# The convolution of the next chunk moved between the two scans, the second C spread early in every turn, the first stretch reordered

## The reference, cut to what matters

```
proj = xn @ W_in + b_in;  x_ssm, x_gate = split(proj)
x_conv = silu(causal depthwise conv of x_ssm, 4 taps, + conv_b)
B, C = split(x_conv @ W_bc + b_bc);  dt = softplus(x_conv @ W_dt + b_dt)
h[t] = h[t-1] * exp(dt[t] * A) + dt[t] * x_conv[t] * B[t]      (16 states per feature)
y[t] = sum over the states of h[t] * C[t] + x_conv[t] * D
mamba = LN((y * silu(x_gate)) @ W_out + b_out + xn)

gates = softmax(xn @ gate_w); the best two of 8 experts, weights normalised
h_e = gelu(LN(xn @ w1_e + b1_e));  y_e = h_e @ w2_e + b2_e
moe = LN(sum of the two weighted y_e + xn)
```

## Time and profile before

| what | value |
|---|---|
| median of 3 runs | 1748.9 us (1748.78 to 1751.86) |
| the profiled execution, its own time | 1749.06 us |
| its span, first to last instruction | 1747.1 us |
| granted TensorE clock, mean | 0.951 of full |
| busy: PE, DVE, ACT, POOL | 1517.9, 1511.7, 1293.8, 1002.6 us |

### The profile page before, as it was taken

The page is one execution under the profiler, slowest core; times in us unless marked ns, Lnnn a source line. Parts: engine busy times, 40 slices in busy tenths (PEclk is TensorE's granted clock), DMA queues, the critical chain, the costliest instruction groups (busy, mean ns, idle before and its releaser), DMA issues.

```text
span 1747.1 us, 27926 instructions
## 1 busy us (share of the span) xinstructions
PE 1517.9 (87%) x6796; PEld 936.7 (54%) x6796; DVE 1511.7 (87%) x2454; ACT 1293.8 (74%) x2431; POOL 1002.6 (57%) x586
## 2 busy tenths in 40 slices
PE   5898549898989999999989898989999999995688
PEld 3665125565555655655556565655566565653233
DVE  5677569999999999999999999999999998941897
ACT  3545358788878787887878787888787878756687
POOL 2677736556656665565656565666665655732233
PEclk9777769999999999999999999999999999999799
DMA  7999643343334333333333433433443433325695
GB/s 227 329 292 347 238 161 83 85 103 98 88 98 107 95 109 90 102 87 98 101 98 90 110 90 100 100 98 87 102 112 87 108 78 91 79 45 140 214 289 172
DMA packets 178468, 228.34 MB, mean 131 GB/s; under 512 B 45967, under 2 KB 145048, under 8 KB 178331
## 3 DMA queue, kind: packets, MB, share of 16 engines
q1 hardware_dynamic: 137422, 166.02, 31.4%
q0 software_dynamic: 25584, 35.54, 10.9%
q10 hardware_dynamic: 15328, 25.20, 4.2%
HBM read 146.17 MB, written 80.53 MB: 130 GB/s over the span
## 4 chain that ended last, share of the span: by engine, by line
DVE 30%; PE 29%; ACT 16%; issue 15%; DMA 5%; ACTq 3%; SPq 1%; DVEq 0%; POOLq 0%
PE psX L1032 6%; DVE area L1358 6%; PE psY L1053 5%; DVE area L1371 4%; DVE area L1367 4%; PE psH L1020 3%; PE psT L1080 3%; ACT area L673 3%; ACT h_T L710 3%; DMA area<-L_attn_x 3%; DVE area L1388 2%; DVE more L1423 2%; PE psT L1008 2%; ACTq L694 2%; PE psT L1110 2%
## 5 line engine op out<-in xcount | busy, mean ns | idle before, releaser
L553 POOL TENSOR_TENSOR area<-area,more 128x1024 f32<-128x1024 f32 x256 | 599.8, 2361 | 490.6 <-DVE area L1367 246.0
L1388 DVE TENSOR_TENSOR area<-area,psD 128x1024 f32<-128x1024 f32 x256 | 310.2, 1212 | 0.5 <-issue 0.2
L1020 PE MATMUL psH<-w_sb,ffn_xT 128*128 x540 | 266.4, 617 | 45.3 <-DVE area L1402 38.0
L537 POOL DMA_INDIRECT expert_d<-y_out,meta x135 | 220.6, 1634 | 80.1 <-ACT y_out L689 33.5
L1053 PE MATMUL psY<-ident,area 128*128 128x128 f32 x2048 | 251.1, 276 | 0.0
L673 ACT ACTIVATE area<-area,A_sb 128x512 f32<-128x512 f32 x256 | 170.0, 712 | 81.8 <-DVE area L1371 43.5
L1053 PEld LDWEIGHTS psY<-ident,area 128*128 128x128 f32 x2048 | 222.7, 141 | 13.6 <-DVE area L1388 0.4
L1032 PE MATMUL psX<-w_sb,h_T 128*128 x720 | 182.8, 399 | 7.5 <-issue 6.5
L667 ACT ACTIVATE psD<-area,A_sb 128x512 f32<-128x512 f32 x256 | 174.8, 683 | 16.5 <-POOL area L544 9.5
L1020 PEld LDWEIGHTS psH<-w_sb,ffn_xT 128*128 128x128 f32 x540 | 96.2, 194 | 149.3 <-issue 149.1
L524 POOL DMA_INDIRECT sorted_x<-area,place x128 | 127.8, 998 | 77.3 <-DVE place L1336 39.8
(11 more groups left out here) (190 smaller groups left out, 2700.1 us busy)
## 6 DMA issues: line engine op xcount, KB each, us to landing
more<-B_rows_d SPq DMA_DIRECT2D x128, 512.0 KB, 4.0
xin<-sorted_x SPq DMA_DIRECT2D x135, 128.0 KB, 2.0
area<-L_attn_x SPq DMA_DIRECT2D x8, 1024.0 KB, 6.8
xnT_d<-w_sb ACTq DMA_DIRECT2D x16, 512.0 KB, 6.5
expert_d<-area ACTq DMA_DIRECT2D x8, 1024.0 KB
ssm_d<-w_sb ACTq DMA_DIRECT2D x16, 512.0 KB
w_sb<-L_ffn_w SPq DMA_DIRECT2D x16, 512.0 KB
more<-ssm_d SPq DMA_DIRECT2D x16, 512.0 KB, 3.9
```

The lines of the kernel that those rows point to most:

```text
L537: pool.indirect_dma_start(out=expert_d, out_offset=bass.IndirectOffsetOnAxis(ap=meta_tok[:, t % RING, :], axis=0), in_=y_out[:, t % 2, :], ...
L553: pool.tensor_tensor(inflow[:, k], dtx, B_rep[par][:, k].rearrange("p (a t) -> p a t", a=1).to_broadcast([P, KD, CHUNK]), ALU.mult).then_i ...
L1020: nc.tensor.matmul(psH[:, :], ffn_xT[:, k, :], w1_sb[:, bass.ds(e, 1), k, :].rearrange("p o h -> p (o h)"), start=(k == 0), stop=False)
L1388: V.tensor_tensor(h, h, C_rep[k].rearrange("p (a t) -> p a t", a=1) .to_broadcast([P, KD, CHUNK]), ALU.mult).then_inc(S[f"hC{k}_done"], 1)
```

## The change

On VectorE `convolve(g, 0)` moves from the end of turn 0 to between `scan0_of` and `scan1_of` of turn 0, and `convolve(g, 1)` with `pad_left` from the end of turn 1 to between `gate` and `scan1_of` of turn 1. On TensorE `spread_C1` (and `transpose_x` in turn 1) take in turns 0 and 1 the place that they have in all others. In the first stretch the ranks come after tile 1 instead of tile 5; `pick` is written behind the other constants and has a semaphore of its own; the memset of `h_T` goes. The scatters are counted in three groups: GpSimd's and VectorE's first scan now wait for tiles below LAST (61 of 64), and only the loads of sorted tokens wait for the rest. SP issues four loads of w2, `store_B(0)`, the padding rows, both `load_B`, and then five loads of w1.

```diff
...
 END_RING = 8
-CONSTS = 22 + 5
+CONSTS = 17 + 5
 
...
         h_norm2 = scan_area.take(HIDDEN)
+        LAST = -(-scan_area.at // ROW)
         scan_more = Carve(sb("more", [P, 7300]), 7300)
...
             xin_loaded xin_T xT_copied h_ready bn_done var_ready hln_ready rstd_ready norm_done hT_done gelu_done
-            y_ready y_copied y_stored pool_consts
+            y_ready y_copied y_stored pool_consts pick_ready scattered_last
             e_bias e_chain e_var e_ln e_root e_scale e_norm e_gain e_gain1 e_sum""".split()
...
             sp.dma_start(xT_in, xnT_d[0].rearrange("p (k t) -> p k t", k=KD)).then_inc(S["xT_loaded"], 16)
+            def store_B(g):
+                sp.wait_ge(S["bc_taken"], g + 1)
+                sp.dma_start(B_rows_d[bass.ds(g, 1)].rearrange("o n t -> (o n) t"), bc_f[0:STATE, :]).then_inc(S["B_stored"], 16)
+
+            def load_B(p, g, pr):
+
+                if pr == 0:
+                    sp.wait_ge(S["B_stored"], 16 * (g + 1))
+                if p >= 2:
+                    sp.wait_ge(S["dbx_done"], 2 * p)
+                sp.dma_start(B_rep[pr % 2], B_rows_d[bass.ds(g, 1), 2 * pr:2 * pr + 2, :].to_broadcast([P, 2, CHUNK])
+                             ).then_inc(S[f"B_loaded{pr % 2}"], 16)
+
+            sp.wait_ge(S["xT_store0"], 16 * TURNS + 16)
+            sp.wait_ge(S["xT_store1"], 16 * TURNS + 16)
+            sp.wait_ge(S["ssm_store0"], 16 * TURNS + 16)
+            sp.wait_ge(S["ssm_store1"], 16 * TURNS + 16)
+            for dst, src in w2_loads[:w2_after]:
+                sp.dma_start(dst, src).then_inc(S["w_ffn"], 16)
+            store_B(0)
             sp.wait_ge(S["pads_found"], 1)
...
                 sp.dma_start(sorted_x[bass.ds(row, P), :], xin[:, :]).then_inc(S["pad_fill"], 16)
+            load_B(0, 0, 0)
+            load_B(1, 0, 1)
             sp.wait_ge(S["tables_ready"], 1)
-            sp.wait_ge(S["xT_store0"], 16 * TURNS + 16)
-            sp.wait_ge(S["xT_store1"], 16 * TURNS + 16)
-            sp.wait_ge(S["ssm_store0"], 16 * TURNS + 16)
-            sp.wait_ge(S["ssm_store1"], 16 * TURNS + 16)
-            for dst, src in w1_loads[:w1_after] + w2_loads[:w2_after]:
+            for dst, src in w1_loads[:w1_after]:
                 sp.dma_start(dst, src).then_inc(S["w_ffn"], 16)
...
 
-            def store_B(g):
-                sp.wait_ge(S["bc_taken"], g + 1)
-                sp.dma_start(B_rows_d[bass.ds(g, 1)].rearrange("o n t -> (o n) t"), bc_f[0:STATE, :]).then_inc(S["B_stored"], 16)
-
-            def load_B(p, g, pr):
-
-                if pr == 0:
-                    sp.wait_ge(S["B_stored"], 16 * (g + 1))
-                if p >= 2:
-                    sp.wait_ge(S["dbx_done"], 2 * p)
-                sp.dma_start(B_rep[pr % 2], B_rows_d[bass.ds(g, 1), 2 * pr:2 * pr + 2, :].to_broadcast([P, 2, CHUNK])
-                             ).then_inc(S[f"B_loaded{pr % 2}"], 16)
-
             def store_mamba(c):
...
             load_ssm(1)
-            store_B(0)
-            load_B(0, 0, 0)
-            load_B(1, 0, 1)
-            sp.wait_ge(S["scattered"], 16 * 2 * (TILES - FIRST))
+            sp.wait_ge(S["scattered"], 16 * 2 * (LAST - FIRST))
+            sp.wait_ge(S["scattered_last"], 16 * 2 * (TILES - LAST))
             sp.wait_ge(S["pad_fill"], 16 * EXPERTS)
...
                 pool.memset([ident, before][k][:, :], 0.0 if k == 0 else 1.0).then_inc(S["pool_consts"], 1)
-            pool.memset(pick[:, :, :], 0.0).then_inc(S["pool_consts"], 1)
-            pool.wait_ge(S["pool_consts"], 5 + 3)
+            pool.wait_ge(S["pool_consts"], 5 + 2)
             pool.affine_select(out=ident[:, :], in_=ident[:, :], compare_op=ALU.not_equal, fill=1.0, base=0,
...
 
-            for r in range(PARTS):
-                pool.wait_ge(S["pool_consts"], 5 + 5 + r)
-                pool.affine_select(out=pick[:, :, :], in_=pick[:, :, :], compare_op=ALU.not_equal, fill=1.0,
-                                   base=-(BC * r + STATE), pattern=[[-1, STATE], [0, P]], channel_multiplier=1
-                                   ).then_inc(S["pool_consts"], 1)
             pool.memset(ones[:, :], 1.0).then_inc(S["pool_consts"], 1)
...
             pool.memset(half_neg[:, :], -0.5).then_inc(S["pool_consts"], 1)
-            pool.memset(h_T[:, :, :, :], 0.0).then_inc(S["pool_consts"], 1)
             pool.memset(ones_e, 1.0).then_inc(S["pool_consts"], 1)
...
             pool.memset(not_first[:, :, 0:1], 0.0).then_inc(S["pool_consts"], 1)
+            pool.memset(pick[:, :, :], 0.0).then_inc(S["pick_ready"], 1)
+            for r in range(PARTS):
+                pool.wait_ge(S["pick_ready"], 1 + r)
+                pool.affine_select(out=pick[:, :, :], in_=pick[:, :, :], compare_op=ALU.not_equal, fill=1.0,
+                                   base=-(BC * r + STATE), pattern=[[-1, STATE], [0, P]], channel_multiplier=1
+                                   ).then_inc(S["pick_ready"], 1)
 
...
                         out=sorted_x, out_offset=bass.IndirectOffsetOnAxis(ap=place[:, i, k:k + 1], axis=0),
-                        in_=row_all[:, i, :], in_offset=None).then_inc(S["scattered_first" if i < FIRST else "scattered"], 16)
+                        in_=row_all[:, i, :], in_offset=None).then_inc(S["scattered_first" if i < FIRST else "scattered" if i < LAST else "scattered_last"], 16)
 
...
             pool.wait_ge(S["zero_fill"], 16 * 2)
-            pool.wait_ge(S["scattered"], 16 * 2 * (TILES - FIRST))
+            pool.wait_ge(S["scattered"], 16 * 2 * (LAST - FIRST))
             pool.wait_ge(S["xn_stored"], 16 * TURNS)
...
 
-            RANKS_AFTER = GROUP - 3
+            RANKS_AFTER = 1
 
...
             pe.wait_ge(S["tables_ready"], 1)
+            pe.wait_ge(S["pick_ready"], 1 + PARTS)
             spread_C0(0, 0, 0, 0)
...
                                 transpose_sum(c)
-                            early_C = pr != CONV_TURN - 1
-                            if early_C:
-                                spread_C1(u + 1, state[1], par)
+                            spread_C1(u + 1, state[1], par)
                             if u >= 2:
                                 down(u - 2)
-                            if not early_C:
-                                spread_C1(u + 1, state[1], par)
                             if pr == 0:
...
                         else:
-                            early_C = pr != CONV_TURN
-                            if early_C:
-                                transpose_x(u + 2)
-                                if go_on:
-                                    spread_C1(u + 1, state[1], par)
+                            transpose_x(u + 2)
+                            if go_on:
+                                spread_C1(u + 1, state[1], par)
                             pe.wait_ge(S["gelu_done"], u)
...
                                 task(TASKS[pr], g)
-                            if not early_C:
-                                transpose_x(u + 2)
-                                spread_C1(u + 1, state[1], par)
                             if u >= 2:
...
             finish_dt(0, 0)
-            dve.wait_ge(S["scattered"], 16 * 2 * (TILES - FIRST))
+            dve.wait_ge(S["scattered"], 16 * 2 * (LAST - FIRST))
             dve.wait_ge(S["xn_stored"], 16 * TURNS)
...
                             gate(c, ahead)
+                        if pr == CONV_TURN - 1 and more:
+                            convolve(g, 0)
+                        if pr == CONV_TURN and more:
+                            convolve(g, 1)
+                            pad_left(half == 0)
                         if pr == BC_TAKEN + 1 and more:
...
                         times_C(u, pr * 2, 0, half)
-                        if pr == CONV_TURN - 1 and more:
-                            convolve(g, 0)
-                        if pr == CONV_TURN and more:
-                            convolve(g, 1)
-                            pad_left(half == 0)
             for u in range(MAMBA_TURNS, FFN_TURNS):
...
```

More of the change, by code:

```diff
@@ L390, in load_B, with load_tile, load_chunk @@
                              ).then_inc(S[f"B_loaded{pr % 2}"], 16)
+            sp.wait_ge(S["xT_store0"], 16 * TURNS + 16)
[5 more added lines that the diff above has]
+            store_B(0)
+            sp.wait_ge(S["pads_found"], 1)
+            for e in range(EXPERTS):
+                row = sp.value_load(pad_row[0:1, e:e + 1], min_val=0, max_val=EXPERTS * REGION * P - P)
+                sp.dma_start(sorted_x[bass.ds(row, P), :], xin[:, :]).then_inc(S["pad_fill"], 16)
+            load_B(0, 0, 0)
+            load_B(1, 0, 1)
+            sp.wait_ge(S["tables_ready"], 1)
+            for dst, src in w1_loads[:w1_after]:
+                sp.dma_start(dst, src).then_inc(S["w_ffn"], 16)
+            def load_tile(t, slot):
+                row = sp.value_load(row_of[0:1, bass.ds(t, 1)], min_val=0, max_val=BLOCKS * P - P)
+                if not (isinstance(t, int) and t == 0):
```

(5 more changed lines are left out.)

14 lines of the change are left out of this document (removed).

## The result

The changed kernel takes 1783.37 us (median of 4 runs, 1777.85 to 1786.75), the kernel before 1749.31 us beside it (4 runs, 1748.78 to 1751.86): a ratio of 1.0189, 95% interval 1.0161 to 1.0217. It is 34 us slower; the forecast was 1785. Its profiled execution took 1786.75 us with a span of 1784.8 us, so it is 3.4 us longer than the median.

What follows compares the result with a forecast made beforehand. VectorE (95.6 of 100 us in the middle) and TensorE (93.6) were both nearly full, so lost slack decides. Base 1749.06, +49 (14 x (1.8 + 1.65) = +48, chunk 0 +1), first stretch -13: 1785 us, range 1770 to 1800.

Steps and rivals of the forecast that it cites:

- The gate: VectorE's gate in turn 1 waits 3.1 us for 0.35; turns 0 and 1 grow +2.0 or +1.6 us, mean 1.8.
- the experiment of the trace: Chunk 15, gated with no convolution between turn 0 and gate, already waits 2.93 us, against 0.35 in chunk 6.
- The tap and the shorter instructions: First convolution waits 0.47 or 0.3 us for the first tap; without GpSimd's product each half shortens 0.67 or 0.98 us.
- Turn 2: `hidden_norm` waits 1.3 us (1.5 in half 1) for ScalarE's root, plus 0.3 in turn 3: 1.65 us per chunk.
- `spread_C1` costs nothing of its own: TensorE's new order: `spread_C1` in turn 1 waits 0.6 us for scans; lateness at turn 2 hidden, otherwise 0.6 us.
- The clock: Rival: TensorE idles 2.6 us before turn 0's `up`, which runs at half clock; +20 us, 1805 us; chance 0.08.
- The front: First stretch gains 13 us, between 0 and 30, from start (-3.5), loop of `places` (-5) and passage (-4.5).
- The start: VectorE begins 3.5 us earlier than 14.08, since the first x at 10.38 decides instead of the constants.
- The passage: From last scatters to first scan: B loads earlier, but tokens and tap hold the rest; -4.5 us, between 0 and -10.
- The faster one: Rival: no gate wait forms between `scan0_of` of turn 1 and gate; shorter convolutions win 24 us, 1712 us; chance 0.1.
- Turn 2 absorbs: Rival: ScalarE and TensorE catch up during the gate's wait, only 1.8 us per chunk lost; 1761 us; chance 0.13.
- the front does nothing: Rival: the first stretch's 8 turns stay at TensorE's pace and tokens arrive as before; 1798 us; chance 0.07.

Runs made afterwards that it cites:

- e10: Changed kernel with ScalarE's gate copy ahead of the decay of state 1 in turn 0 instead of behind it: 1782.23 us.
- e8: Changed kernel plus three useless 128x512 matmuls on TensorE ahead of the `up` of turn 1: reported median 1777.89 us, profiled execution 1771.43 us.
- e9: Changed kernel with both convolution halves put back to their old places, keeping the new front and early `spread_C1`: 1778.46 us.
- e1: Changed kernel with both convolution halves and `spread_C1` put back, so only the first stretch and passage are changed: 1732.57 us.
- e2: Kernel before with only the two convolution halves moved between the scans, `spread_C1` late, first stretch as before: 1799.75 us.
- e6: Against e1: `convolve(g, 0)` moved between `scan0_of` of turn 1 and the gate, and `transpose_sum` ahead of `transpose_h` and `transpose_x`: 1715.85 us.
- e7: Changed kernel with `convolve(g, 1)` back at the end of turn 1 and `spread_C1` back in its late places: 1776.47 us.
- e5: Changed kernel with `transpose_sum` ahead of `transpose_h` and `transpose_x` on TensorE in turn 0: 1758.05 us.

## Why the prediction was right

**The gate.** Right in size and place. Forecast 3.1 us in chunks 1 to 15, found 2.93 and 3.10 in chunks at the full clock and up to 3.96 with the clock down. The start-to-start sum for turns 0 and 1, +2.0 and +1.6 us, came out at +1.85 (26.31 for 24.46) and +1.54 (26.34 for 24.80) at the full clock. Reading as the experiment of the trace was the step that carried this. The list of the path was right in what stands in it and wrong in one link: the gate copy is no part of it (e10), since the decay behind it waits for `times_C` anyway.

**The tap and the shorter instructions.** Forecast 0.47 and 0.3 us for the wait, found 0.50 and 0.35. All 96 convolution instructions take at most 0.754 us; the saving of 0.67 and 0.98 us is real. The Trainium skill, SBUF — State Buffer, section "SBUF: two separate sides", agrees with both ends: the same instruction is longer only where a GpSimd product runs (30 of the 96 before, each beside such a product, and none after).

**Turn 2.** The term of +1.65 us is mis-sized. The root arrives 7.73 us after the start of turn 2 (762.54 + 0.20 - 755.01, forecast 7.9), the norm waits 1.00 or 1.05 us where 1.3 or 1.5 stood. At the full clock turn 2 takes 9.6 us for 8.5, so +1.1, and the later turns of an even chunk of e8 are 0.2 us longer in sum, where I had 0.3 for turn 3. With it the forecast for the order of work, 3.45 us per chunk, is 2.8 in e8.

**`spread_C1` costs nothing of its own.** For the changed kernel the words and the reason held. At the full clock (e8, chunk 6) it waits 0.34 us for the scans of turn 2, forecast 0.6, and `add_up` ends at 757.67, 0.45 us before `scan0_of` of turn 3 at 758.12. In that turn VectorE waits 0.99 us for the root. Without that cover the scan would wait 0.5 to 0.6 us, which is the 0.6 of the prediction (an estimate from these rows). What failed is what I made of it afterwards, in the expectation for e9: with conv1 at its old place TensorE stops 3.26 us at `spread_C1`, the scan of turn 3 waits 2.2 to 4.9 us, and early C costs 46 us where 0 to 8 were expected. The part that the order of work explains is again some 0.6 us per chunk; I had left out that the engine runs at half the clock after such a stop. The prediction does not say that the two edits hang on each other, and they do.

**The clock.** I gave 0.08 to a rival that in a smaller form took place. It put 2.6 us of idle time ahead of the `up` of turn 0 and took 20 us. TensorE idles 1.45 and 0.33 us there; the 3 us stand ahead of the `up` of turn 1. The lower clock is there in 13 of 14 chunks of the profiled execution, in four of them over both `up` as in chunk 6, in three over that of turn 1 alone, in six over work between them, where the gate then waits up to 3.96 us, and what it adds is 0.8 us per chunk, 11 us (e8). Part of it is hidden: the slow `up` of turn 0 ends at 742.66, before gelu at 743.43. Much of what shows is `scan0_of` waiting for `add_up`, 10.7 us; its 4.5 us in the kernel before, which also has a low stretch in five of these 14 chunks, were a sign that the prediction passed over. The Trainium skill, TensorE: Matmul & The Clock Gate, section "HAM oscillation — how this bites in real kernels", gave the warning that repeated idle gaps make the array start slow, and the rows of chunk 6 agree (3.43 us after 3.04 us idle), though not every chunk of these kernels does (last section); my argument against it, that chunk 15 shows no such row, was worth little: in chunk 15 of the kernel before TensorE's longest idle time around the gate is 1.23 us and the next `up` waits 0.74, and the 3.04 us ahead of the `up` of turn 1 arise only with a convolution in that turn. Some 0.65 too much on the order and some 0.8 left out for the clock cancelled: the total per chunk, 3.55, lies beside 3.45 by two errors of opposite sign. The mechanism was right; that the number fits so closely is luck.

**The front.** Forecast -13, measured -16.2 (e1). The start: 14.08 to 11.15, -2.9 for -3.5. In the loop the last `places` begins at 184.8 (e1 183.4) instead of 192.2, so -4.5 to -6 behind the start for -5. The passage gave more than the -4.5 forecast: the first tap moved from 233.1 to 219.8 (e1 218.4), and chunk 1 of e1 starts 16.3 us earlier (297.2 for 313.5), so 7 to 9 us are the passage's. The first scan came at 214.27, not near 220, and its `scan1_of` ended 11.4 us earlier, as forecast. One profiled execution doesn't tell more, since the same front starts its first scan anywhere from 210.9 to 220.5 us in the kernels here.

**The rivals.** The faster one is refuted where it was placed (e2: +51), though its saving is what e6 earns. "Turn 2 absorbs" is refuted by the 1.0 us of the norm in every kernel with conv1 moved and early C (in e2 in six of 14 chunks, in the other eight `times_C` waits for `spread_C1` instead), "the front does nothing" by e1.

## What to carry to other kernels

A block of work on the bound engine is also cover: moved ahead of the instruction that a path starts from, it lengthens the wait at the path's end by its own length, and moved behind it, just ahead of the waiting instruction, it fills the wait. Look in the trace for a turn in which the block is missing; it prices the move. And before a waiting instruction is moved forward on an in-order engine, ask which scan or copy it waits for and what stands ahead of that: here one such edit cost 46 us alone, and 14 us together with the move of what stood ahead (5 of them in the chunks). Most of the 46 us, by the estimate above, is the lower clock after the stop: a stop on TensorE can cost far more than the order of work alone says.

## What was not expected of the hardware

TensorE fell to its lower clock (1.2 of 2.4 GHz) in nearly every chunk while it was busy for 88% of the time (1340 to 1440 us): `up` took 3.43 us for 1.98 after 3.04 us of idle time. Of the kernel before, no wait of TensorE between 400 and 1400 us is longer than 1.8 us. Three useless products of 128x512 in the hole, 2.74 us, brought the longest wait back to 1.8 us, and in the profiled execution the full clock held over all 14 chunks, for a gain of 0.8 us in each.

The length of a single wait does not decide it, though. In e2 and e7 (`up` of turn 1 in chunk 13 of e2; `up` of turn 0 in chunk 3 of e7, and the longest wait of TensorE in e7, 400 to 1400 us):
```profile
1371.14 1.98 PE L1020 MATMUL psH<-w_sb,ffn_xT 128*128 x4 [3.40 <-DVE area L1402]
...
482.30 3.62 PE L1023 MATMUL psH<-w_sb,ffn_xT 128*128 x4 [0.31 <-ACT ffn_xT L685]
...
PE psH L1023 <- DVE area L1406: 26.5, 22, 1.7
```
In e2 chunks 12 to 14 have waits of 3.1 to 3.4 us and no stretch at the lower clock. In e7 no wait is over 1.8 us, and ten of 14 chunks have one. In e5, whose `up` of turn 1 waits 1.1 to 1.4 us where the clock is up, six chunks are slow. Which idle times the chip reacts to is not settled here.
